# A fused attention and edge-filter kernel on one core: the q part of a 5x5 convolution as three products of split operands, the weight split moved to the 14th head, the first head's tap matrix built earlier

## The reference, cut to what matters

```
q, k, v = h @ wq.T, h @ wk.T, h @ wv.T
qkv = concat(q, k, v)
dw = conv(qkv, dw_kernel, 5x5, one filter per channel)
pw = conv(dw, pw_kernel, 1x1, groups of 8 channels)
qkv_all = concat(qkv, pw)           # 64 plain heads and 64 convolved heads of 8
scores = value_pad . relu(key)      # per head
out = scores . relu(query), divided by its last row
y = batchnorm(conv1x1(out, proj_kernel)) + x
```

## Time and profile before

| what | value |
|---|---|
| median of 3 runs | 5162.94 us (5160.89 to 5172.66) |
| the profiled execution, its own time | 5166.08 us |
| span of the profiled execution | 5164.3 us |
| PE busy | 4887.3 us, 95% of the span |
| PEld busy | 3443.6 us |
| DVE / ACT / POOL busy | 2579.4 / 2023.0 / 1223.6 us |
| mean granted TensorE clock | 0.977 |

### The profile page before, as it was taken

The page is one execution under the profiler, slowest core; times in us unless marked ns, Lnnn a source line. Parts: engine busy times, 40 slices in busy tenths (PEclk is TensorE's granted clock), DMA queues, the critical chain, the costliest instruction groups (busy, mean ns, idle before and its releaser), DMA issues. The chain is left out here.

```text
span 5164.3 us, 65339 instructions
## 1 busy us (share of the span) xinstructions
PE 4887.3 (95%) x22760; PEld 3443.6 (67%) x22760; DVE 2579.4 (50%) x3635; ACT 2023.0 (39%) x3671; POOL 1223.6 (24%) x1030
## 2 busy tenths in 40 slices
PE   8999999999999999999999997899999989998968
PEld 7887887887887888888888883344344434443423
DVE  3334334334334333333334321786688578848865
ACT  3333333333333333333333320454555455545545
POOL 2442342342342342342342330000300020011003
PEclk9999999999999999999999998999999999999969
DMA  6665666665665665665666654443334344434313
GB/s 184 197 216 203 198 211 203 198 212 202 198 213 203 198 215 203 198 214 203 198 213 203 203 185 170 139 147 123 138 123 155 108 147 131 143 118 145 110 34 116
DMA packets 390808, 893.04 MB, mean 173 GB/s; under 512 B 33488, under 2 KB 66512, under 8 KB 388240
## 3 DMA queue, kind: packets, MB, share of 16 engines
q1 hardware_dynamic: 390544, 889.18, 52.2%
HBM read 588.74 MB, written 300.32 MB: 172 GB/s over the span
## 5 line engine op out<-in xcount | busy, mean ns | idle before, releaser
L733 POOL TENSOR_TENSOR toeplitz<-taps 128x512 f32<-128x512 f32 x768 | 889.2, 1186 | 959.1 <-PE bank L441 959.1
L441 PEld LDWEIGHTS bank<-toeplitz,columns 128*128 128x128 f32 x8192 | 954.4, 192 | 13.8
L441 PE MATMUL bank<-toeplitz,columns 128*128 128x128 f32 x8192 | 955.7, 275 | 0.0
L1039 PE MATMUL bank<-att,w_proj 128*128 128x512 f32 x2048 | 906.2, 597 | 47.7 <-DMA att<-att_dram 36.6
L1039 PEld LDWEIGHTS bank<-att,w_proj 128*128 128x128 f32 x2048 | 392.1, 192 | 543.6 <-issue 505.1
L356 PE MATMUL bank<-x_hi,w_hi 128*128 128x512 f32 x1536 | 610.8, 398 | 17.1 <-DVE x_lo L600 17.1
L1383 POOL TENSOR_TENSOR centred<-centred,x_out 128x512 f32<-128x512 f32 x128 | 164.6, 1321 | 1910.2 <-ACT centred L1191 1910.2
L358 PE MATMUL bank<-x_lo,w_hi 128*128 128x512 f32 x1536 | 600.9, 391 | 0.0
L1052 PE MATMUL bank<-edge,w_branch 128*128 128x512 f32 x1024 | 503.2, 639 | 102.5 <-ACT edge L1142 102.5
L357 PE MATMUL bank<-x_hi,w_lo 128*128 128x512 f32 x1536 | 599.5, 390 | 0.0
L671 DVE TENSOR_SCALAR ckey_t<-bank 128x256 f32<-128x256 f32 x256 | 107.5, 420 | 872.0 <-PE bank L441 872.0
(11 more groups left out here) (115 smaller groups left out, 5618.9 us busy)
## 6 DMA issues: line engine op xcount, KB each, us to landing
x_sb<-in_x_tiled SPq DMA_DIRECT2D x128, 1024.0 KB, 6.4
tiles_dram<-tiles SPq DMA_DIRECT2D x128, 867.0 KB, 6.7
loaded<-tiles_dram SPq DMA_DIRECT2D x256, 433.5 KB, 4.0
inverse<-inverse_dram SPq DMA_DIRECT2D x256, 256.0 KB, 4.8
att_dram<-out_sb SPq DMA_DIRECT2D x256, 256.0 KB, 4.1
att<-att_dram SPq DMA_DIRECT2D x64, 1024.0 KB, 6.2
xb<-x_dram SPq DMA_DIRECT2D x128, 330.0 KB, 3.1
x_out<-in_x_pad SPq DMA_DIRECT2D x32, 1056.0 KB, 5.2
```

Source lines behind the costliest of these rows:

```text
L441: last = nc.tensor.matmul(bank[:, v * M:(v + 1) * M], columns[:, h % 2, t - T_K, v + b, a * HT:(a + TO) * HT], w[:, t, d, :], start=(d == ...
L733: last = nc.gpsimd.tensor_tensor(toeplitz[:, h % 2, t, :].rearrange("p (d o r) -> p d o r", o=HD, r=PL), tap, point, ALU.mult)
L1039: last = nc.tensor.matmul(P_BANKS[m][:, :], w_proj[:, i * HALF + k, m * P:(m + 1) * P], att[:, i, k, :], start=(i == 0 and k == 0), stop=( ...
```

## The change

The q product of each head is done like the projections: the head's q tile and its q matrix are split into a rounded part and a remainder, and 12 F32R matmuls of 256 columns take the place of the 4 F32 ones. ACT makes the rounded parts (`round_q`, 289 columns, and `round_taps`, 512 columns), DVE the remainders (`split_q`, `split_taps`), in place. The rounded tiles `q_hi` and `tq_hi` are single. `split_weights` moves from behind head 7 to behind head 13. POOL's two builds in `plain` move from chunks 3 and 5 to chunks 0 and 3, and the first head's q matrix is split in chunk 1. `score_d` becomes one band in a row of 240 columns, read through shifted windows, so one DVE operation writes it.

```diff
-                    pe.wait_ge(tiles_loaded[h % LR], 16 * (SH // LR) * it + 16 * (h // LR) + 16)
-                    pe.wait_ge(toeplitz_ready, SH * it + h + 1)
+                    pe.wait_ge(q_split, SH * it + h + 1)
+                    pe.wait_ge(tq_split, SH * it + h + 1)
...
-                        last = nc.tensor.matmul(q_bank[0:M, 0:TT], w[:, T_Q, d, :], x_q[:, a:a + TO, b:b + TO],
-                                                start=(d == 0), stop=(d == len(SHIFTS) - 1))
+                        high, low = x_hi_q[:, a:a + TO, b:b + TO], x_lo_q[:, a:a + TO, b:b + TO]
+                        narrow = tq_lo[:, h % 2, T_Q, d * M:(d + 1) * M]
+                        nc.tensor.matmul(q_bank[0:M, 0:TT], wide[:, d, :], high, start=(d == 0), stop=False)
+                        nc.tensor.matmul(q_bank[0:M, 0:TT], narrow, high, start=False, stop=False)
+                        last = nc.tensor.matmul(q_bank[0:M, 0:TT], wide[:, d, :], low, start=False, stop=(d == len(SHIFTS) - 1))
                     last.then_inc(cready[T_Q], 1)
 
+                    pe.wait_ge(toeplitz_ready, SH * it + h + 1)
...
+                def round_q(it, h):
+                    act.wait_ge(tiles_loaded[h % LR], 16 * (SH // LR) * it + 16 * (h // LR) + 16)
+                    copy(q_hi[:, :], loaded[:, h % LR, T_Q, :]).then_inc(q_rounded, 1)
+
+                def round_taps(it, h):
+                    act.wait_ge(tq_built, SH * it + h + 1)
+                    copy(tq_hi[:, :], toeplitz[:, h % 2, T_Q, :]).then_inc(tq_rounded, 1)
...
                         nc.scalar.activation(q_stage[:, h % 2, :], CONV_BANKS[T_Q][h % 2][0:M, 0:TT], ACT.Relu).then_inc(cevac[T_Q], 1)
+                        if h + 1 < SH:
+                            round_q(it, h + 1)
+                            round_taps(it, h + 1)
...
-                    apart, last = P + SH, (NCH - 1) * (P + SH)
-                    nc.vector.tensor_scalar(score_d[:, 0:last].rearrange("p (j s) -> p j s", s=apart)[:, :, 0:SH],
-                                            mask[:, None, :].to_broadcast([P, NCH - 1, SH]), key_sum[:, 0:1], None, ALU.mult)
-                    nc.vector.tensor_scalar(score_d[:, last:last + SH], mask[:, :], key_sum[:, 0:1], None,
+                    nc.vector.tensor_scalar(score_d[:, P - SH:P], mask[:, :], key_sum[:, 0:1], None,
                                             ALU.mult).then_inc(sums_placed, 1)
...
+                def split_q(it, h):
+                    dve.wait_ge(q_rounded, SH * it + h + 1)
+                    nc.vector.tensor_tensor(q_lo[:, h % LR, T_Q, :], loaded[:, h % LR, T_Q, :], q_hi[:, :].bitcast(F32), ALU.subtract).then_inc(q_split, 1)
+
+                def split_taps(it, h):
+                    dve.wait_ge(tq_rounded, SH * it + h + 1)
+                    nc.vector.tensor_tensor(tq_lo[:, h % 2, T_Q, :], toeplitz[:, h % 2, T_Q, :], tq_hi[:, :].bitcast(F32), ALU.subtract).then_inc(tq_split, 1)
...
                     for h in range(SH):
+                        if h + 1 < SH:
+                            split_q(it, h + 1)
+                            split_taps(it, h + 1)
                         dve.wait_ge(cready[T_K], SH * it + h + 1)
...
-                        if more and h == 7:
+                        if more and h == SH - 3:
                             split_weights(it + 1)
...
-                        if j in (3, 5):
-                            build(it, j // 2 - 1)
+                        if j in (0, 3):
+                            build(it, j // 3)
```

More of the change, by code:

```diff
@@ L83, in attention @@
         cvalue_t = sb("cvalue_t", [P, HV * PL, P + 1])
-        loaded = sb("loaded", [P, LR, 3, TN])
+        with nc.sbuf_tensor("loaded", [P, LR, 3, TN], F32) as loaded:
+            pass
+        q_lo = ctx.enter_context(nc.sbuf_tensor("q_lo", [P, LR, 3, TN], F32R))
         columns = sb("columns", [P, 2, 2, HV + 1, TG * HT])
-        toeplitz = sb("toeplitz", [P, 2, 3, len(SHIFTS) * M])
+        with nc.sbuf_tensor("toeplitz", [P, 2, 3, len(SHIFTS) * M], F32) as toeplitz:
+            pass
+        tq_lo = ctx.enter_context(nc.sbuf_tensor("tq_lo", [P, 2, 3, len(SHIFTS) * M], F32R))
+        tq_hi = ctx.enter_context(nc.sbuf_tensor("tq_hi", [P, len(SHIFTS) * M], F32R))
+        q_hi = ctx.enter_context(nc.sbuf_tensor("q_hi", [P, TN], F32R))
         q_stage = sb("q_stage", [M, 2, TT])
         score_n = sb("score_n", [P, P])
-        score_d = sb("score_d", [P, NCH * P])
+        score_d = sb("score_d", [P, 2 * P - SH])
         score_t = sb("score_t", [P, P])
@@ L143, in attention @@
         toeplitz_ready = sem("toeplitz_ready")
+        tq_built = sem("toeplitz_q_built")
+        tq_rounded = sem("toeplitz_q_rounded")
+        tq_split = sem("toeplitz_q_split")
+        q_rounded = sem("q_tiles_rounded")
+        q_split = sem("q_tiles_split")
         cready = [sem(f"conv_{n}_ready") for n in "qk"]
@@ L397, in denominate @@
                     for j in range(NCH):
-                        last = nc.tensor.matmul(DEN_BANK[:, :], score_d[:, j * P:(j + 1) * P], rows((relu_q, relu_c)[half], j),
+                        last = nc.tensor.matmul(DEN_BANK[:, :], score_d[:, P - SH * (j + 1):2 * P - SH * (j + 1)], rows((relu_q, relu_c)[half], j),
                                                 start=(j == 0), stop=(j == NCH - 1))
@@ L424, in conv_head @@
                     q_bank, k_bank, v_bank = (of[h % 2] for of in CONV_BANKS)
[L425 to L427 removed]
+                    wide = tq_hi[:, :].rearrange("p (d m) -> p d m", m=M)
+                    x_hi_q = q_hi[:, :].rearrange("p (a c) -> p a c", c=TG)
+                    x_lo_q = q_lo[:, h % LR, T_Q, :].rearrange("p (a c) -> p a c", c=TG)
+                    pe.wait_ge(q_split, SH * it + h + 1)
+                    pe.wait_ge(tq_split, SH * it + h + 1)
                     if h >= 2:
@@ L523, in plain @@
                             round_x(it, j + 1)
+                        if j == 1:
+                            round_taps(it, 0)
                         key(it, j)
@@ L538, in conv @@
                 def conv(it, last):
+                    round_q(it, 0)
                     gather(it, 0)
@@ L661, in plain @@
                         compress(it, j)
+                        if j == 1:
+                            split_taps(it, 0)
                     keys_by_position(it, NCH - 2)
@@ L664, in plain @@
                     mask_scores(it, 0)
+                    split_q(it, 0)
                     invert(it, 0)
@@ L734, in build @@
                             toeplitz[:, h % 2, t, :].rearrange("p (d o r) -> p d o r", o=HD, r=PL), tap, point, ALU.mult)
+                        if t == T_Q:
+                            last.then_inc(tq_built, 1)
                     last.then_inc(toeplitz_ready, 1)
```

1 line of the change is left out of this document (removed).

## The result

The changed kernel takes 5126.2 us (median of 5 runs, 5115.5 to 5132.8), the kernel before 5167.4 us on the same chip (5 runs, 5160.9 to 5174.8). The ratio is 0.9916, with a 95% interval of 0.9897 to 0.9936: 41 us or 0.8% faster.

A forecast was written before the change was run, and what follows sets the result against it. PE was taken as the bound, busy 3024 of 3110 us in the first layer. Terms -51 - 9 - 3 + 5 + 10 + 6 + 10 = -32 us gave 5134, or 5131 as median; whole range 5082 to 5175.

The forecast's parts named there:

- the change of type: PE's switch from F32 to F32R matmuls, forecast at 0.093 us per head; costing nothing or 0.2 would show the prediction wrong.
- A: Each head's q product on PE: 12 F32R matmuls at 0.120 us plus 0.093, 1.53 us in place of 1.73; -51 us.
- rival 3: F32R pairs of 256 columns are slower than estimated: 5223 us at 0.150, 5435 if loads don't overlap; chance 0.16.
- B: Head 9's wait of 0.61 us for POOL's matrix goes, with the weight split elsewhere; 15 rounds, -9 us.
- C: Between last score and denominator one of two DVE operations goes: 0.20 us in 16 rounds and once at the end, -3 us.
- D: Head 1's q product waits for DVE subtractions queued behind the reciprocal: +0.3 us in 16 rounds, +5 us.
- E: Head 15's q product waits for DVE subtractions queued behind the weight split: 0.7 us in 15 rounds, +10 us.
- F: Other heads: DVE and POOL slow each other in the eight heads with divisions, 0.05 us per head, +6 us.
- G: In `plain`, POOL's first build slows DVE's remainder for chunk 1, so PE waits 0.6 us in 15 rounds; +10 us.
- the second: Rival: DVE and POOL operations with SBUF operands exclude each other wholly, eating the gain; 5165 us, chance 0.14.

The follow-up runs named there:

- the mask alone: The kernel before with nothing but the new score_d, one DVE operation in place of two and denominator weights read through shifted windows: ratio 0.9991.
- four moves: Changed kernel with builds behind chunks 3 and 5, reciprocal behind head 1's subtractions, weight split behind head 14, x's loads behind heads 11 and 13: 5095.5 us.

## Why the prediction was right

The time was 5126 where 5131 was forecast, and 41 us below the kernel before where 32 were forecast. One of the prediction's own signs of being wrong came all the same: the change of type costs nothing. By its own steps:

- **A, the q product.** Right in its main mechanism, 12 short records in place of 8 long ones, each at a cost on top of its columns near that of the projections. It has two errors that nearly cancel, and that is luck: the pair is 0.125 and not 0.120 (+15 us), and the 0.093 for a change of type doesn't exist (-24 us). Forecast 1.53 us for q and -51; measured 1.50 and a period 0.23 shorter, 256 x 0.23 = -59. The second error was in the reading: the earlier trace rows show a first record 0.32 ahead of the next, and I took the gap for time spent. A distance between starts of unlike matmuls isn't a duration; the period from one q product to the next would have said so. The Trainium skill ("TensorE: Matmul & The Clock Gate", Part 2, Back-to-back issue gap and LDWEIGHTS) gives N/2.4 + 2.5 ns for a warm matmul by itself, 109 ns for 256 columns, and 107 ns for a load of 128 weight columns. Side by side they would take 109 ns; the trace has 125 for the pair. The Trainium skill (the same page, Part 3, What overlaps and what doesn't) lets a weight load overlap a running matmul only when the row group differs, which would give the 0.219 of rival 3. The 0.125 here speaks against it.
- **B, head 9.** The wait is gone. I took the long period against 5.30, 0.61; that was one round. The mean over heads 8 and 9 is 0.36 + 0.07, so -6.5 and not -9.
- **C, the mask.** The wait is 0.2 shorter in a round, as forecast: -3. That is read from the trace; the time of the mask alone doesn't tell it from nothing.
- **D, head 1.** The reciprocal stands ahead of two subtractions: `tq_lo` ends 0.15 before PE starts, and head 0's period is 5.77 with the reciprocal there and 5.48 with it behind, 0.29 (forecast 0.3), +5.
- **E, head 15.** Forecast 0.7, measured 5.76 - 5.07 = 0.69, +10. Inside it two terms were off: the cast started earlier and took 0.94 and not 1.76, and the subtractions took 2.77 and not 1.07. Beside the build, DVE's 1.76 + 0.45 + 0.68 = 2.89 us of work and POOL's 3.08 took 569.70 - 564.32 = 5.38, a factor of 0.90 where I had 0.86 from the earlier trace rows.
- **F, the other heads.** Forecast 0.05 in eight heads; measured 0.15 ahead of head 8, 0.04 ahead of head 11 and nothing elsewhere, +3. The cause was argued wrong: I looked for the port, and it is the inverse's transfer behind x's, which DVE's queue hands on to PE.
- **G, chunk 1.** Forecast 0.6. The first record of chunk 1 starts 0.43 later, but it is an early-dated one. By the length of `plain`, 105.8 with the build there and 105.2 without, it is 0.6 in 15 rounds, +9.

That makes -42. Three half-clock intervals in the rounds of this execution, where the one before had none behind `plain`, and two late remainders in chunk 7 of single rounds give +5 and +2: -35, against -35.7 in the trace. The medians differ by 41; other executions of the changed kernel had a clock of up to 0.980 where the profiled one has 0.977, so less time at half clock, in either layer, is the likely reason, which only their own traces could show. The clock was no term of my sum, and it is worth as much as D.

Of the rivals, the second's rule is visible: `q_lo` takes 831 ns in the mean and 450 alone. Means over the first layer:

```profile
L676 DVE TENSOR_TENSOR q_lo<-loaded,q_hi 128x289 fp32r<-128x289 f32 x256 | 212.8, 831 | 381.3 <-ACT q_hi L502 381.3
...
L680 DVE TENSOR_TENSOR tq_lo<-toeplitz,tq_hi 128x512 fp32r<-128x512 f32 x256 | 225.6, 881 | 2.2
```

The Trainium skill ("SBUF — State Buffer", Who interferes with whom) states a lock between such instructions, and the lengthened rows agree. But 381 us of idle time stand ahead of `q_lo` in all, so most heads had room for it.

## What to carry to other kernels

When an engine that isn't the bottleneck gets new work that the bottleneck needs, price its place in the queue and not its busy share: DVE was busy for half of the layer, and all that it cost was behind one slow operation or one late transfer, which four moves of order took back (23 us of the first layer, beside the 36 that the change took from it). Work that PE needs next goes ahead of reciprocals, large splits and anything that waits for a DMA. Read the cost of a change on PE from periods between like instructions. A wait can cost more than its length: here 3.7 us of waiting ahead of full work cost 1.7 us more in clock. And before a gain is put down to an edit, see whether it stands in the part of the program that the edit touches.

## What was not expected of the hardware

- An F32R pair of 256 columns takes 0.125 us and one of 512 columns 0.227: 0.01 to 0.02 us on top of the columns at 2.4 GHz. The 256 columns are read as 16 out of each 17 of the tile; whether that has a part in the 0.02 isn't shown. Three of them beat two F32 passes (0.375 against 0.433) and four don't.
- The first F32R record behind F32 matmuls is dated 0.08 us early in the heads, and 0.4 early where a head follows products of 512 columns (0.03 us behind the last of them, where 0.43 lay before), so such a head's period reads 0.3 too long.
- After 3.66 us without work PE ran on at full clock for less than 1 us and then at half for 3.4 us. After waits of 1.5, 0.8 and 0.8 us within 5 us the same came in some rounds and not in others.
- With matmuls that fill the idle time there was no half clock in one execution, but gaps appeared about 8 us later in the weight loads (0.35 us in one round). They aren't explained.
- The second layer, which no edit touches, took 2059.8 and 2060.7 us in two executions with the four moves and 2071 in those of the change and of the kernel before, with 196 to 200 us at half clock in place of 227.
